# Attention maxima: for one of four query tiles, two key chunks are joined by a score difference

## What is computed

```python
x = x + attn_a(layernorm(x)); x = x + ffn(layernorm(x))
x = x + attn_b(layernorm(x)); x = x + ffn(layernorm(x))

# an attention: 16 heads of 16, n = 4096, causal
sim = einsum('bhid,bhjd->bhij', q, k) / sqrt(16)
sim = where(causal_mask, -max, sim)
exp_sim = exp(sim - max(sim, axis=-1))
denom = sum(exp_sim, axis=-1) + exp(denom_bias)      # layer a; b has no such term
out = einsum('bhij,bhjd->bhid', exp_sim / denom, v)  # then out @ Wo.T (+ bo in a)
```

## Time and profile before

| | |
|---|---|
| median of three runs | 4868.34 us |
| profiled execution | 4872.37 us, span 4870.6 us |
| mean granted TensorE clock | 0.964 of full speed |
| TensorE, matmuls | 4460.6 us busy, 40558 instructions |
| VectorE | 4097.5 us, 4711 |
| ScalarE | 3124.9 us, 5863 |
| GpSimd | 1214.8 us, 1201 |

### The profile page before, as it was taken

How to read it: one execution, slowest core, us unless ns; L and a number is a source line. 1 busy time by engine, 2 the same in 40 slices (tenths; PEclk the granted TensorE clock), 3 DMA queues, 4 the chain that set the end, 5 groups by cost and what they waited for, 6 DMA issues and landing times. The chain is left out here.

```text
span 4870.6 us, 97833 instructions
## 1 busy us (share of the span) xinstructions
PE 4460.6 (92%) x40558; PEld 1971.9 (40%) x40558; DVE 4097.5 (84%) x4711; ACT 3124.9 (64%) x5863; POOL 1214.8 (25%) x1201
## 2 busy tenths in 40 slices
PE   5889999999999799899988999999999997998998
PEld 3322223322224465556652222232222344654566
DVE  5599998999985898778847999989998858885887
ACT  1377898888997344334433789888899964443443
POOL 2000001100002477544401000011000015774443
PEclk9699999999999799999987999999999997999999
DMA  4300000000000000220031000000000000004000
GB/s 149 76 21 8 2 15 15 8 15 8 2 2 5 18 1 1 66 74 1 0 81 65 19 4 2 15 15 15 15 2 2 2 13 9 1 1 139 10 13 13
DMA packets 73656, 112.31 MB, mean 23 GB/s; under 512 B 12389, under 2 KB 56677, under 8 KB 68965
## 3 DMA queue, kind: packets, MB, share of 16 engines
q1 hardware_dynamic: 68634, 99.95, 6.2%
q0 software_dynamic: 4608, 6.50, 1.0%
HBM read 73.70 MB, written 31.47 MB: 22 GB/s over the span
## 5 line engine op out<-in xcount | busy, mean ns | idle before, releaser
L879 DVE TENSOR_REDUCE b_att_mx<-ps 128x2 f32<-128x1024 f32 (+3 forms) x1152 | 1228.3, 1130 | 105.9 <-PE ps L732 80.5
L879 DVE TENSOR_REDUCE a_att_mx<-ps 128x2 f32<-128x1024 f32 (+3 forms) x1152 | 1228.2, 1130 | 104.4 <-PE ps L732 79.2
L836 ACT ACTIVATE a_att_pt<-ps 128x512 f32<-128x512 f32 (+3 forms) x2304 | 1146.7, 560 | 210.6 <-PE ps L768 181.0
L836 ACT ACTIVATE b_att_pt<-ps 128x512 f32<-128x512 f32 (+3 forms) x2304 | 1147.1, 560 | 208.3 <-PE ps L768 178.7
L787 PE MATMUL ps<-a_att_pt,a_v 128*17 128x256 f32 (+1 forms) x8704 | 672.6, 381 | 10.8 <-ACT a_att_osb L823 9.8
L787 PE MATMUL ps<-b_att_pt,b_v 128*17 128x256 f32 (+1 forms) x8704 | 672.0, 381 | 10.7 <-ACT b_att_osb L823 9.7
L768 PE MATMUL ps<-a_q,a_k 51*128 51x512 f16 (+3 forms) x1152 | 363.3, 370 | 0.3 <-ACT a_att_pt L836 0.2
L768 PE MATMUL ps<-b_q,b_k 51*128 51x512 f16 (+3 forms) x1152 | 362.7, 369 | 0.2 <-ACT b_att_pt L836 0.2
L713 POOL TENSOR_SCALAR_AFFINE_SELECT a_att_pt<-a_att_pt 128x512 f32<-128x512 f32 x128 | 81.3, 635 | 1123.2 <-ACT a_att_pt L836 1110.9
L713 POOL TENSOR_SCALAR_AFFINE_SELECT b_att_pt<-b_att_pt 128x512 f32<-128x512 f32 x128 | 81.4, 636 | 1122.9 <-ACT b_att_pt L836 1110.6
L768 PE MATMUL ps<-b_att_q,b_att_k 51*128 51x512 f16 (+3 forms) x1152 | 338.7, 365 | 1.1 <-ACT b_att_pt L836 0.6
(11 more groups left out here) (313 smaller groups left out, 7318.2 us busy)
## 6 DMA issues: line engine op xcount, KB each, us to landing
f_mix_ct<-in_expert_w SPq DMA_DIRECT2D x64, 256.0 KB, 5.1
g_mix_ct<-in_expert_w SPq DMA_DIRECT2D x64, 256.0 KB, 4.6
a_parts_q<-a_qkv_cut SPq DMA_DIRECT2D x24, 256.0 KB, 2.9
a_parts_k<-a_qkv_cut SPq DMA_DIRECT2D x24, 256.0 KB, 2.8
b_parts_q<-b_qkv_cut SPq DMA_DIRECT2D x24, 256.0 KB, 2.9
b_parts_k<-b_qkv_cut SPq DMA_DIRECT2D x24, 256.0 KB, 2.8
x<-in_x SPq DMA_DIRECT2D x1, 4096.0 KB, 21.8
out<-x SPq DMA_DIRECT2D x8, 512.0 KB, 2.9
```

The costliest lines, as they stand in the source:

```text
L836: act.activation(pt[:, s % PT_RING, i, 0:width], ps[:, at:at + width], ACT.Exp, scale=unscale).then_inc(pt_ready, 1)
L879: dve.tensor_reduce(mx[u % 2][:, h:h + 2, t, c], both, AX.X, ALU.max).then_inc(ring_read, 1)
```

## The change

For the first query tile of a group (t = 0), whole key chunks are taken in couples 2j and 2j + 1, as many as `coupled(g) = g // 2`; a chunk left over and the masked end stay as they were, and so do tiles 1 to 3. For each couple and pair of heads two score pairs (`S`) become:

- an item `X` (`rise`): TensorE makes the scores of chunk 2j minus those of chunk 2j + 1, by adding a matmul with the negated queries (`negq`) to one with the queries, for both heads, in two banks of the exponentials' ring; it waits for ScalarE's reads like any tile there. ScalarE writes the positive part (Relu) to `risen` in SBUF, a ring of two pairs;
- an item `Y`, two items later: TensorE makes the scores of chunk 2j + 1 in VectorE's ring as before; VectorE adds `risen` to them and takes the maximum, one operation per head over 512 elements (`tensor_tensor_reduce`). b + max(a - b, 0) is max(a, b).

`X` and `Y` take the places of two `S` in the order. `ACT_TILES` numbers what ScalarE reads, exponentials and differences together, and the semaphore `st_read` replaces `pt_ready`. GpSimd negates the first tile of each group's queries, four operations per quad. The closing reduction is split in two, since t = 0 has fewer values. The constant rows are made once, in the first phase, kept in DRAM (`minus_rows`) and loaded from there.

The core of the diff:

```diff
-            pool.memset(minus[:, :], -1.0 / M_SCALE).then_inc(minus_set, 1)
-            pool.wait_ge(minus_set, 1)
...
+def coupled(g):
+    return g // 2
...
 def score_items(u):
     g = UNITS[u][1]
-    whole = [(pair, t, c, BANK) for t in range(KB) for c in range(g) for pair in range(2)]
+    whole = [("S", pair, t, c, BANK) for t in range(KB) for c in range(g) for pair in range(2) if t or c // 2 >= coupled(g)]
...
+    couples = [(pair, 2 * j) for j in range(coupled(g)) for pair in range(2)]
+    order = list(rest)
+    for j, (pair, c) in reversed(list(enumerate(couples))):
+        at = (2 * j + 1) * len(rest) // (2 * len(couples))
+        order.insert(at + 2, ("Y", pair, 0, c + 1, BANK))
+        order.insert(at, ("X", pair, 0, c, BANK))
...
+ACT_TILES = [what for tile, items in enumerate(ITEMS_AFTER)
+             for what in [(*i[:2], i[2] + h, *i[3:]) for i in items if i[0] == "X" and i[2] % 2 == 0 for h in (1, 0)]
+             + [("E", tile)] * (tile < 4 * NS)]
...
+            def negate(quad):
+                if quad:
+                    pool.wait_ge(st_read, ACT_AT[RISES[LAST_RISE[quad - 1]]] + 1)
+                wait(pool, p_loaded[quad % 2], LOADS * ((quad + 1) // 2))
+                for pair in range(2):
+                    for r in (0, P // 2):
+                        own = q[quad % 2][pair][r:r + ROWS, :].rearrange("p (g n) -> p g n", g=G)[:, NEG_FROM:G, 0:P]
+                        pool.tensor_scalar(negq[r:r + ROWS, pair, :, :], own, -1.0, None, ALU.mult).then_inc(negated, 1)
+                    pool.wait_ge(negated, 4 * quad + 2 * pair + 2)
...
+            def rise(what):
+                _, u, h, t, c, width = what
+                quad, g = UNITS[u]
+                pe.wait_ge(negated, 4 * (quad + 1))
+                for part in range(2):
+                    for i in (1, 0):
+                        n = ACT_AT[("X", u, h + i, t, c, width)]
+                        r, at = 64 * i, ST + (n % ST_RING) * BANK
+                        if part == 0:
+                            wait(pe, st_read, n - ST_RING + 1)
+                            pe.matmul(ps[:, at:at + BANK], q[quad % 2][h // 2][r:r + ROWS, KB * g * P:(KB * g + 1) * P],
+                                      k[quad % 2][h // 2][r:r + ROWS, c * BANK:(c + 1) * BANK], start=True, stop=False)
+                        else:
+                            pe.matmul(ps[:, at:at + BANK], negq[r:r + ROWS, h // 2, g - NEG_FROM, :],
+                                      k[quad % 2][h // 2][r:r + ROWS, (c + 1) * BANK:(c + 2) * BANK],
+                                      start=False, stop=True).then_inc(st_ready, 1)
...
+                    act.wait_ge(st_ready, n + 1)
+                    act.activation(risen[:, j % RISEN, h % 2, :], ps[:, at:at + BANK], ACT.Relu).then_inc(st_read, 1)
...
+                if kind == "Y":
+                    over = "X", u, h, t, c - 1, width
+                    dve.wait_ge(st_read, ACT_AT[over] + 1)
+                    for i in range(2):
+                        up = risen[:, RISE_AT[over] % RISEN, i, :]
+                        last = dve.tensor_tensor_reduce(up, ps[:, at + i * BANK:at + (i + 1) * BANK], up, 1.0, NEG, ALU.add, ALU.max,
+                                                        mx[u % 2][:, h + i, t, c // 2:c // 2 + 1])
+                    last.then_inc(ring_read, 1)
...
-                    dve.tensor_reduce(mfull[u % 2][:, :, :], mx[u % 2][:, :, :, 0:g + 1], AX.X, ALU.max).then_inc(m_full, 1)
+                    dve.tensor_reduce(mfull[u % 2][:, :, 0], mx[u % 2][:, :, 0, 0:g + 1 - coupled(g)], AX.X, ALU.max)
+                    dve.tensor_reduce(mfull[u % 2][:, :, 1:KB], mx[u % 2][:, :, 1:KB, 0:g + 1], AX.X, ALU.max).then_inc(m_full, 1)
```

More of the change, by code:

```diff
@@ L138, in load_and_cut @@
         ones_row = sb("ones_row", [1, 2, N], F16)
+        minus = sb("minus", [3, N], F16)
         scales = Scales(sb, "phi")
@@ L178, in _ @@
             pool.memset(ones_row[:, 1, :], 0.0).then_inc(row_made, 1)
+            pool.memset(minus[:, :], -1.0 / M_SCALE).then_inc(row_made, 1)
             pool.wait_ge(cleared, 1)
@@ L535, in is_diagonal, with place_of @@
     return kb >= KB * UNITS[u][1]
+def coupled(g):
+    return g // 2
+def place_of(g, t, c):
+    return c if t else (c // 2 if c // 2 < coupled(g) else c - coupled(g))
 def score_items(u):
     g = UNITS[u][1]
-    whole = [(pair, t, c, BANK) for t in range(KB) for c in range(g) for pair in range(2)]
-    ends = [(pair, t, g, P * (t + 1)) for pair in range(2) for t in range(KB)]
-    order = [item for j, end in enumerate(ends) for item in (*whole[j * g:j * g + (g + 1) // 2], end, *whole[j * g + (g + 1) // 2:(j + 1) * g])]
-    return [("S", u, 2 * pair + h, t, c, width) for pair, t, c, width in order for h in (1, 0)]
+    whole = [("S", pair, t, c, BANK) for t in range(KB) for c in range(g) for pair in range(2) if t or c // 2 >= coupled(g)]
+    ends = [("S", pair, t, g, P * (t + 1)) for pair in range(2) for t in range(KB)]
+    cuts = [j * len(whole) // len(ends) for j in range(len(ends) + 1)]
+    rest = []
+    for j, end in enumerate(ends):
+        middle = (cuts[j] + cuts[j + 1] + 1) // 2
+        rest += [*whole[cuts[j]:middle], end, *whole[middle:cuts[j + 1]]]
+    couples = [(pair, 2 * j) for j in range(coupled(g)) for pair in range(2)]
[4 more added lines that the diff above has]
+        order.insert(at, ("X", pair, 0, c, BANK))
+    return [(kind, u, 2 * pair + h, t, c, width) for kind, pair, t, c, width in order for h in (1, 0)]
 def lead_line():
@@ L600, with attention @@
 ITEMS_AFTER = ring_schedule()
-RING_ITEMS = [what for items in ITEMS_AFTER for what in items if what[0] != "S" or what[2] % 2 == 0]
+RING_ITEMS = [what for items in ITEMS_AFTER for what in items if what[0] in "MT" or (what[0] in "SY" and what[2] % 2 == 0)]
 ITEM_AT = {what: n for n, what in enumerate(RING_ITEMS)}
 ITEM_STEP = {what: (tile - 1) // 4 for tile, items in enumerate(ITEMS_AFTER) for what in items}
-LAST_SCORE = [max(n for n, what in enumerate(RING_ITEMS) if what[0] == "S" and what[1] == u) for u in range(NU)]
+LAST_SCORE = [max(n for n, what in enumerate(RING_ITEMS) if what[0] in "SY" and what[1] == u) for u in range(NU)]
+ACT_TILES = [what for tile, items in enumerate(ITEMS_AFTER)
+             for what in [(*i[:2], i[2] + h, *i[3:]) for i in items if i[0] == "X" and i[2] % 2 == 0 for h in (1, 0)]
+             + [("E", tile)] * (tile < 4 * NS)]
+ACT_AT = {what: n for n, what in enumerate(ACT_TILES)}
+RISES = [what for what in ACT_TILES if what[0] == "X" and what[2] % 2 == 0]
+RISE_AT = {what: j for j, what in enumerate(RISES)}
+LAST_RISE = [max((j for j, what in enumerate(RISES) if UNITS[what[1]][0] == quad)) for quad in range(QUADS)]
+NEG_FROM = [g for g in range(G) if coupled(g)][0]
+RISEN = 2
 MAXIMA_AFTER = [ITEM_STEP[RING_ITEMS[LAST_SCORE[u]]] for u in range(NU)]
 PLACED = 8
-def attention(nc, m, ps, tag, layer, v, attn, parts_q, parts_k, denom_bias, first_q, first_k):
+def attention(nc, m, ps, tag, layer, v, attn, parts_q, parts_k, denom_bias, first_q, first_k, minus_rows):
     with phase_of(nc, tag) as (ctx, sem, sb):
```

88 lines of the change are left out of this document (52 added, 36 removed).

## The result

The changed kernel takes 5066.6 us, the median of four runs (5060.2 to 5076.2), beside 4869.5 us for the kernel before (4862.5 to 4872.4): a ratio of 1.041, 95% interval 1.039 to 1.043. That is 197 us more, or 1.03 us for each of the 192 couples of the two layers. The prediction had 4996 us, 128 more, in a range of 4840 to 5100. The profiled execution took 5064.4 us with a span of 5062.7.

The account below looks back on a forecast made before the run. VectorE was taken to bound units 7 to 23, TensorE and ScalarE the last units. Terms of 29 + 18 + 12 + 5 = 64 us a layer, 128 in both, gave 4996 us as a median, range 4840 to 5100.

Parts of the forecast that it names:

- The stall: TensorE's second difference tile waits for ScalarE's read of tile n, the half step's first exponential tile: 1.01 us more.
- The last stage: Units 24 to 31 of an attention, paced by TensorE and ScalarE: nothing hides the wait, 18 us a layer.
- slow operation: Rival: VectorE's two-operand operation takes 1183 ns, adding 132 us a layer, 5133 us as a median; chance 0.12.
- the slack that hides it: Units 7 to 23: TensorE's room of 0.045 us a half step, 0.48 us per couple, hides part of the wait.
- Middle stage: Units 7 to 23, VectorE setting the pace: 0.53 us left per couple, 54 couples, 29 us a layer.
- the negations at nothing: GpSimd's 16 query negations a layer, about 0.95 us each: nothing taken, 8 us as high end.
- the first stage: Units 0 to 6: VectorE idles some 1.3 us per difference, net +0.5 us, 24 couples, 12 us a layer.
- VectorE's operation: Each add-and-maximum over 512 elements takes 0.75 us: 1.50 a couple replacing 2.26, 0.76 saved.
- The closing reductions: VectorE's closing reduction becomes two: 0.15 us more for some 25 units, 5 us a layer.
- fits on average and is not the bound: ScalarE's two more tiles per couple in units 7 to 23: 11.9 us of work in 12.2 us.
- The covered burst: Rival: ScalarE reads early, TensorE pays only its extra slot: -22 us a layer, 4824 us as a median; chance 0.18.
- Table loads: Rival: Relu isn't in Exp's table, so each couple costs two loads of 1.28 us more, 5490 us; chance 0.03.

Follow-up runs that it names:

- experiment 2: Changed kernel with GpSimd's four negations per quad split into eight half-size pieces, each behind a step's selection: 5038.3 us, ratio 1.035.
- Experiment 11: Kernel before, with VectorE reading one column instead of 512 of each couple's first chunk, those maxima left out: 4831.9 us, ratio 0.993.
- experiment 4: Changed kernel with each couple's second chunk reduced plainly, first-chunk maxima left out, and ScalarE's positive part covering one column: 5057.1 us, ratio 1.039.
- experiment 8: Changed kernel with negations spread and the difference written to VectorE's ring of pairs instead of the exponentials' ring: 4965.5 us, ratio 1.020.
- experiment 1: Changed kernel with the two heads' difference tiles issued in two different half steps, two score pairs apart: 5092.2 us, ratio 1.046.
- experiment 5: Changed kernel with difference tiles in two half steps, score pairs between them taking heads in swapped order, negations spread: 5003.5 us, ratio 1.028.

## Why the prediction was right, and where it wasn't

**Right: the mechanism and the side.** The stall was forecast as ScalarE's read of tile n, 1.01 us in a half step with a difference, and the trace has 1.06 (2.16 instead of 1.10), with the weight load of line 793 waiting 0.51 us for ScalarE where 0.4 to 0.6 was named. Reductions of all widths fell from 1152 to 960 a layer (of the widest, which the rows show, from 960 to 767 in the stretch), their idle time rose to 260 us, 192 reads of 0.59 us came up on ScalarE. The last stage, with nothing to hide behind, was put at 18 us and came to 19.1. Layer by layer, 64 us were forecast; without the negations' blocks (experiment 2) the attentions took 86 and 83 us more than before.

**Luck, in part: the range.** Its upper end, 5100, had been left open for a slow operation on VectorE. That didn't come; what brought the time up there were mainly the two terms that follow.

**Wrong: the slack that hides it, the term that failed.** The step "Middle stage: before the change TensorE had 0.045 x 10.7 = 0.48 us per couple" took the mean half step, 1.145 us, less TensorE's 1.10, as room in every half step. Of the 640 half steps of that stage before the change the median is 1.097 us: TensorE's own. The mean is above it mainly by 167 half steps over 1.15 us, and 136 of these lie within a few steps of a unit border or a diagonal. Experiment 11 measures the room at 8.7 us for 54 couples, 0.16 each. With the stall at 1.06 the middle stage comes, as an estimate from these, to 1.06 x 54 - 8.7 = 48.5 us instead of the 29 forecast, and experiment 2, without the negations' blocks, has 49.0. The earlier trace rows said so: TensorE 709.85 of 733 us, VectorE 698.11. "VectorE sets it" was read off the pace of VectorE's operations, 1.13 us, which an engine also shows that is handed a pair each 1.10 to 1.15 us.

**Wrong: the negations at nothing.** The high end was 8 us; they cost 26 to 28. Each takes 2.19 us (8.74 / 4), not 0.95: the scaling went by elements per partition from an operation on 128 partitions and another type. The place of the trouble, the diagonal's selection behind them, was named, its price was not: 3.88 us of TensorE's standstill, and the clock after it.

**Too low: the first stage.** Forecast 12 us, 17.6 in experiment 2, where the stage lasts 333.9 us with VectorE busy 275.3, against 316.3 and 299.3 before. So each of its 25 couples brings 1.66 us of idle time and spares 0.96 of work: the idle time was forecast as 1.3.

**Too high, with little effect: VectorE's operation.** Taken as 0.75 us; one follows another by 0.61 us (572.74 to 573.35), its accumulator read of 0.08 us in it. The Trainium skill (VectorE: DVE Perf Modes, section "Two Vector instructions with no wait between them") says that such an operation is two instructions; the trace agrees, at 0.08 us instead of the 0.15 that the prediction priced it with, and it delays nothing that can be seen. A couple costs VectorE 1.22 us instead of 2.26. The closing reductions take 6.4 + 5.4 us a layer instead of 7.3, 4.5 more, forecast 5.

**Wrong though it did no harm: ScalarE "fits on average and is not the bound".** True of the average, 11.9 of 12.2 us. But its two reads come in one burst between exponentials that TensorE awaits, and cost 89 us once the bank wait no longer hides them. The bank wait that the prediction named makes the whole stall by itself: with ScalarE's reads short the half step stayed at 2.16 to 2.19 us (experiment 4). But it covers a second wait which the prediction put at nothing, and that one comes out when the first is taken away: half of the cost was left.

**The rivals.** The covered burst wanted a half step under 1.58 us; experiment 8 reaches 1.32 in the half step itself and still loses in a later one. Even the full relief of experiment 11 gives 4832 us, so its 4824 was out of reach. The slow operation fell with the 0.61 us above. Table loads: none in the attention beyond the two that were there before; that relu shares exp's table is so in this trace.

## What to carry to other kernels

The slack that an edit can use is not the mean of a stage less the floor of the next engine. Take the distribution: if the median period is another engine's floor already, there is no slack, and the mean is made by a few places that the edit doesn't touch. The cheapest probe is to spare the suspected engine its work for nothing, in a kernel that leaves it out; here one run would have said that about 33 us is all that VectorE's relief can win, before a word of the change was written.

Work moved to an engine that has room on average still arrives as a burst. Ask which consumer waits for the instruction behind it, and which buffer its late read holds: in this kernel the same microsecond came up as a bank wait, as a late exponential, or as a late place in the ring, depending on the order.

## What the runs showed of the hardware that I had not expected

- Two matmuls of 512 columns on the same 64 rows of the array start 0.21 us apart, on different halves together (experiment 1). A half step with four score matmuls in one half and one in the other takes 1.67 us there, with three and two 1.31 us at best (experiment 5), with three and three 1.32 (experiment 8).
- GpSimd's negation of 48x768 f16 takes 2.19 us, of 48x384 1.16 us, where its selection on 128x512 f32 takes 0.64.
- After 3.88 us without a matmul TensorE's half steps take 1.96 us instead of 1.10 for some 6 us.
